# A perceiver layer's cross attention: the second of two freed context units loaded by four whole DMAs instead of some fourteen pieces

## What is computed

```python
x = x + xattn(layernorm(x), ctx)          # ctx: 8 x 1601 x 2048
x = x + attn(layernorm(x), w_q, w_k, w_v, w_o)
x = x + ffn(layernorm(x), A_w, B_w, Wq_w, keys)

def xattn(query, key):
    a = einsum('bqd,bkd->bqk', query, key)
    return einsum('bqk,bkd->bqd', softmax(a, axis=-1), key)
```

## Time and profile before

| | us |
|---|---|
| median of 3 runs | 1615.14 |
| lowest, highest run | 1612.77, 1623.99 |
| the profiled execution, its own time | 1612.68 |
| its span | 1610.9 |

### The profile page before, as it was taken

How to read it: one execution, slowest core, us unless ns; L and a number is a source line. 1 busy time by engine, 2 the same in 40 slices (tenths; PEclk the granted TensorE clock), 3 DMA queues, 4 the chain that set the end, 5 groups by cost and what they waited for, 6 DMA issues and landing times.

```text
span 1610.9 us, 24088 instructions
## 1 busy us (share of the span) xinstructions
PE 1478.6 (92%) x9593; PEld 1044.2 (65%) x9593; DVE 777.1 (48%) x1095; ACT 505.8 (31%) x698; POOL 625.3 (39%) x282
## 2 busy tenths in 40 slices
PE   1698988888889699999999999999999999999999
PEld 0233333333333388888888888888888888878777
DVE  2456646647655320446544644644465440357323
ACT  1032433433433422332423423323323332222221
POOL 0031422413405324366466564663663663430000
PEclk9899999999899799999999999999999999999999
DMA  9999899989985423233133233323331343230023
GB/s 233 247 216 227 203 255 255 216 252 254 226 238 123 139 102 108 79 105 105 56 106 98 78 104 104 102 85 99 104 104 55 106 152 105 79 105 1 29 76 131
DMA packets 182222, 219.96 MB, mean 137 GB/s; under 512 B 9488, under 2 KB 107792, under 8 KB 179504
## 3 DMA queue, kind: packets, MB, share of 16 engines
q1 hardware_dynamic: 182144, 218.87, 50.1%
HBM read 207.82 MB, written 10.49 MB: 136 GB/s over the span
## 4 chain that ended last, share of the span: by engine, by line
PE 76%; DMA 8%; DVE 6%; SPq 5%; issue 2%; ACT 2%; DVEq 0%; POOL 0%; ACTq 0%
PE ps L729 15%; PE ps L731 14%; PE ps L730 14%; PE ps L666 11%; DMA xa_raw<-in_ctx 8%; SPq L305 5%; PE ps L1769 5%; PE ps L1771 5%; PE ps L1770 5%; DVE xa_kt L520 2%; PE ps L642 2%; PE ps L1709 2%; PE ps L1862 1%; DVE xa_kt L524 1%; PE ps L1734 1%
## 5 line engine op out<-in xcount | busy, mean ns | idle before, releaser
L729 PE MATMUL ps<-h_hi,w_hi 128*128 128x512 f32 x800 | 315.4, 394 | 1.2 <-DVE h_lo L1425 1.1
L731 PE MATMUL ps<-h_hi,w_lo 128*128 128x512 f32 x800 | 311.7, 390 | 0.0
L730 PE MATMUL ps<-h_lo,w_hi 128*128 128x512 f32 x800 | 311.5, 389 | 0.0
L1157 POOL TENSOR_TENSOR w_lo<-raw,w_hi 128x2048 fp32r<-128x2048 f32 (+1 forms) x52 | 212.7, 4095 | 254.4 <-ACT w_hi L1222 213.8
L474 POOL TENSOR_TENSOR xa_x<-xa_x,xa_tmp 64x512 f32<-64x512 f32 x120 | 150.3, 1269 | 360.0 <-ACT xa_tmp L403 348.1
L622 PE MATMUL ps<-xa_kt,xa_q_t 128*64 128x416 f32 (+2 forms) x1024 | 211.1, 557 | 78.7 <-DVE xa_kt L520 56.4
L520 DVE STREAM_TRANSPOSE xa_kt<-xa_raw 128x832 f32<-128x832 f32 (+1 forms) x208 | 193.9, 995 | 158.4 <-PE ps L622 102.9
L622 PEld LDWEIGHTS ps<-xa_kt,xa_q_t 128*64 128x64 f32 x1024 | 71.8, 146 | 208.1 <-issue 134.5
L666 PE MATMUL ps<-xa_raw,xa_e_t 32*64 32x512 f32 (+1 forms) x3264 | 184.1, 593 | 0.0
L729 PEld LDWEIGHTS ps<-h_hi,w_hi 128*128 128x128 f32 x800 | 150.2, 188 | 36.4 <-issue 6.4
L1513 DVE TENSOR_TENSOR rows<-rows,ps 128x512 f32<-128x512 f32 x168 | 115.5, 688 | 116.3 <-PE ps L1771 116.3
(11 more groups left out here) (222 smaller groups left out, 1894.3 us busy)
## 6 DMA issues: line engine op xcount, KB each, us to landing
xa_raw<-in_ctx SPq DMA_DIRECT2D x128, 320.0 KB, 8.5
xa_raw<-in_ctx SPq DMA_DIRECT2D x144, 256.0 KB, 11.0
raw<-in_L_attn_w_q SPq DMA_DIRECT2D x32, 1024.0 KB, 5.9
raw<-in_L_attn_w_o SPq DMA_DIRECT2D x30, 1024.0 KB, 5.0
xa_raw<-in_ctx SPq DMA_DIRECT2D x64, 192.0 KB
xa_raw<-in_ctx SPq DMA_DIRECT2D x64, 128.0 KB
raw<-in_L_attn_w_k SPq DMA_DIRECT2D x8, 1024.0 KB, 5.2
raw<-in_L_attn_w_v SPq DMA_DIRECT2D x8, 1024.0 KB, 5.2
```

The source lines that it names most:

```text
L729: pe.matmul(out, hi, mov_hi, start=first, stop=False)
L730: pe.matmul(out, hi, mov_lo, start=False, stop=False)
L731: return pe.matmul(out, lo, mov_hi, start=False, stop=last)
L1157: pool.tensor_tensor(w_lo[:, n % 2, part], raw[:, n % 2, part], w_hi[:, n % 2, part].bitcast(F32), ALU.subtract).then_inc(w_lo_done, 1)
```

## The change

- Only units on side 1 (odd `u`) are still loaded in three pieces. A unit on side 0 (even `u`) is loaded whole: one DMA for each quadrant, four in all, counted on the third piece's semaphore. It is issued when TensorE is through with side 1 of the half batch. The order of the two (`2s+5`, then `2s+6`) stays.
- The first five units at the start follow the same rule.
- `load_rows` at half batches 5 and 9 now stands behind both units, no longer between them.
- The loader takes an engine and a queue; queue 1 (ScalarE) has no quadrants, so ScalarE issues no DMA. But the waits that go ahead of the loads are also in ScalarE's program: ahead of the copies 1, 4 and 7 of `first_half_moved` for thirds 0, 1, 2 of side 0, and ahead of `evacuate`.

```diff
-QUAD_ORDER = (0, 2, 1, 3)
+QUEUE_QUADS = ((0, 2, 1, 3), ())
+REFILL_AT = (1, 4, 7)
...
+def pieces_of(u):
+    return range(NPIECE) if u % SIDES else range(NPIECE - 1, NPIECE)
...
+def piece_runs(u, g, i):
+    n = BLOCKS[u // SIDES % HALVES]
+    if not u % SIDES:
+        return [(0, n)]
...
         for u in range(PLACES):
-            for g in range(NPIECE):
-                load_unit_piece(u, g)
+            for g in pieces_of(u):
+                load_unit_piece(sp, 0, u, g)
...
-            for a in range(SIDES):
-                u = SIDES * s + a + PLACES
-                for g in range(NPIECE):
-                    if u < UNITS:
-                        products(sp, s, g, [a])
-                        load_unit_piece(u, g)
...
+            for g in range(NPIECE):
+                u = SIDES * s + PLACES
+                if u < UNITS:
+                    products(sp, s, g, [0])
+                    load_unit_piece(sp, 0, u, g)
...
+            if SIDES * s + 1 + PLACES < UNITS:
+                products(sp, s, sides=[1])
+                load_unit_piece(sp, 0, SIDES * s + 1 + PLACES, NPIECE - 1)
+            if s >= 5 and (s - 5) % 4 == 0 and s < 10:
+                sp.wait_ge(norm_stored, 16 * ((s - 5) // 4 + 1))
+                load_rows((s - 5) // 4 + 2)
...
+        def refill(s, g):
+            u = SIDES * s + PLACES
+            if u < UNITS:
+                products(act, s, g, [0])
+                load_unit_piece(act, 1, u, g)
+
+        def refill_whole(s):
+            u = SIDES * s + 1 + PLACES
+            if u < UNITS:
+                products(act, s, sides=[1])
+                load_unit_piece(act, 1, u, NPIECE - 1)
...
             for k in range(A_OPS):
+                if k in REFILL_AT:
+                    refill(HALVES * b + 1, REFILL_AT.index(k))
...
         def evacuate(s):
             b, x = divmod(s, HALVES)
+            if x == 0:
+                for g in range(NPIECE):
+                    refill(s, g)
+            refill_whole(s)
             products(act, s)
```

More of the change, by code:

```diff
@@ L67, in place @@
     return (u + 2) % PLACES
-def piece_runs(x, g, i):
-    n = BLOCKS[x]
+def pieces_of(u):
[4 more added lines that the diff above has]
+        return [(0, n)]
     j0, j1 = PIECES[g] + i, min(PIECES[g + 1], n) + i
@@ L85, in piece_loads @@
     for v in range(u % PLACES, u + 1, PLACES):
-        n += sum(len(piece_runs(v // SIDES % HALVES, g, i)) for i in range(QUADRANTS))
+        n += sum(len(piece_runs(v, g, i)) for i in range(QUADRANTS) if g in pieces_of(v))
         n += g == NPIECE - 1 and has_left(v)
@@ L294, in part_of, with load_unit_piece @@
         return own(b) if k % 2 == 0 else other(b)
-    def cross_sync(sp, aside):
[L297 to L310, removed]
+    def load_unit_piece(eng, queue, u, g):
+        s, a = divmod(u, SIDES)
+        b, x = divmod(s, HALVES)
+        at = UNIT * place(u)
+        for i in QUEUE_QUADS[queue]:
+            for j0, j1 in piece_runs(u, g, i):
+                k0 = KEY0[x] + a * COLS[x] + SQ * j0
+                src = ctx[b, k0:k0 + SQ * (j1 - j0), i * 512:(i + 1) * 512].rearrange("(k c) n -> c k n", c=SQ)
+                eng.dma_start(raw[quadrant(i), at + j0:at + j1, :], src).then_inc(raw_in[place(u)][g], 16)
+        if queue == 0 and g == NPIECE - 1 and has_left(u):
+            if u == 2:
+                eng.wait_ge(left_clear, 1)
+            left = ctx[b, LEFT_KEY, :].rearrange("(i n) -> i n", i=QUADRANTS)
+            eng.dma_start(raw[0:P:SQ, at + LEFT_BLOCK, :], left).then_inc(raw_in[place(u)][g], 16)
+    def cross_sync(sp, aside):
         def load_rows(t):
@@ L325, in cross_sync @@
                 sp.dma_start(x1_norm[t * P:(t + 1) * P, :], xs[t % 2][:]).then_inc(norm_stored, 16)
-            for a in range(SIDES):
-                u = SIDES * s + a + PLACES
-                for g in range(NPIECE):
-                    if u < UNITS:
-                        products(sp, s, g, [a])
-                        load_unit_piece(u, g)
[L332 to L338, removed]
+            for g in range(NPIECE):
[3 more added lines that the diff above has]
+                    load_unit_piece(sp, 0, u, g)
+                if g == 0 and s >= 4 and s % 4 == 0:
+                    t = s // 4 - 1
+                    sp.wait_ge(pool_op, BATCH_OPS * (2 * t + 2))
+                    sp.dma_start(x1[t * P:(t + 1) * P, :], xs[t % 2][:]).then_inc(x1_stored, 16)
+            if SIDES * s + 1 + PLACES < UNITS:
[4 more added lines that the diff above has]
+                load_rows((s - 5) // 4 + 2)
             if s == STAGES - 3:
@@ L427, in last_moved @@
                                scale=g_b[other(b), :]).then_inc(tmp_in, 1)
+        for u in range(PLACES):
+            for g in pieces_of(u):
+                load_unit_piece(act, 1, u, g)
         normalize_rows(0)
```

## The result

| | us |
|---|---|
| kernel before, median of 4 runs | 1615.6 (1612.77 to 1623.99) |
| changed kernel, median of 4 runs | 1636.34 (1633.32 to 1638.16) |
| ratio | 1.0118, 95% interval 1.0077 to 1.0158 |
| profiled execution of the changed kernel, own time | 1638.16 |

The change costs 1.2%, about 19 us by the ratio. The prediction was 1621.8 with a range to 1630, and 0.09 for a loss of over 1%: right that it is slower, and too small by more than half.

A forecast was written before the change was run, and what follows sets the result against it. The prediction took the cross attention's loop to be bound by the landing of unit `2s+5`. It summed 1612.7 + 4.7 (rows of x) + 4.4 (clock) = 1621.8 us, other terms 0, range 1611 to 1630.

The forecast's parts named there:

- What bounds the cross attention: Cross attention: the loop closes through a DMA, since the last third of unit `2s+5` must land before VectorE's transposes.
- the sign that half batches 0 to 5 take the same time: Half batches 0 to 5 together take as long as before; otherwise a load taken as hidden is on the path.
- Fewer DMAs: SyncE's queue: 464 issues become 296, 73 us less issue time, taken at 0 because nothing on the path waits.
- Rows of `x` behind the whole unit: Half batches 6 and 10: rows land later, TensorE's queries and VectorE's transposes wait, 2.2 and 2.5 us, 4.7 together.
- The clock: TensorE in half batches 6 and 10: clock falls to 0.50 after the gaps, 2.2 us at each place, 4.4.
- ScalarE's waits: ScalarE's copies 1, 4 and 7 wait for freed thirds; taken as covered, 0, or 8 us if not.
- Speed of a whole unit: Even units loaded whole: 237 GB/s, 14.4 us for 13 blocks, taken as no change.
- Rival 3: Whole units load slower: at 200 GB/s some 18 us, 1640; decides from 217 GB/s, over 1% slower; chance 0.08.
- The second rival: Whole units load faster: at 301 GB/s 1606.7 to 1611 us, by the skill's figure 1604; chance 0.10.

The follow-up runs named there:

- e9: e6 with quadrants 0 and 1 on SyncE's queue, 2 and 3 on ScalarE's, and ScalarE's start loads reordered around its normalizations: 1571.89 us, ratio 0.9701.
- e10: e7 with the first and second thirds of the odd units also loaded in two rounds of quadrants each: 1589.90 us, ratio 0.9832.
- e11: e5 with the quadrants in the order 0, 1, 2, 3 instead of 0, 2, 1, 3, odd units too: 1636.08 us, ratio 1.0101.
- e5: e1 with each even unit in 12 DMAs, third by third, the quadrants alternating within each third: 1615.88 us, ratio 0.9998.
- e4: e1 with each even unit in 12 DMAs, a quadrant's three one behind the other: 1623.74 us, ratio 1.0039.
- e1: The changed kernel with the x rows at half batches 5 and 9 loaded between the two units again: 1619.94 us, ratio 1.0022.
- e2: The kernel before with only the x rows at half batches 5 and 9 moved behind both units: 1625.02 us, ratio 1.0059.
- e3: e1 without the waits that the change put into ScalarE's program: 1622.75 us, ratio 1.0048.
- e12: The changed kernel with each even unit in 12 DMAs, third by third, instead of 4: 1628.33 us, ratio 1.0067.
- e8: e1 reading other context bytes, rows 6 KB apart and from all four columns, written to the same places: 1617.01 us, ratio 1.0009.
- e7: e5 with the even units loaded in runs of two blocks, 28 or 24 DMAs a unit: 1609.99 us, ratio 0.9967.
- e6: e1 with quadrants 0 and 2 loaded from SyncE's queue and 1 and 3 from ScalarE's: 1633.14 us, ratio 1.0108.

## Why the prediction was right and wrong

- **What bounds the cross attention:** right. Faster landings shorten it at once (e9, e10), slower ones lengthen it (e11). But the sign that half batches 0 to 5 take the same time did not hold: in the chains the first values start 3.7 us later and those of half batch 5 5.7 us later (233.34 for 227.69). The 3.7 are the whole units of the start, which are on the path: e5, whose quadrants alternate, starts its first values within 0.2 us of before. What adds the other 2 us up to half batch 5 stays open.
- **Fewer DMAs, taken at 0:** right. The line now has 296 issues. e4 loads an even unit in the order of e1 with three times as many DMAs, and runs at the same rate.
- **Rows of `x` behind the whole unit, 4.7 + 4.4 us:** right in place and order, too small by some 5 us. The idle times were read too small: TensorE stood 8.50 and 7.23 us in e2, where I had 5.9 and 5.0. That is 4.8 us more, with the cover already used up, and makes the sum 13.9; the trace of e2 has 14.3. The failed reading is the landing. I took the rows to land 1.4 us ahead of the first DMA of the next third, since they are ahead of it in the queue. In half batch 6 of e2 that DMA was issued at 263.45 and landed 6.7 us later, at 270.2, and the rows at 270.97, behind it; why a load can land behind a DMA that was issued after it stays open. That the median of e2 gives 9.5 us and the forecast 9.1 is no confirmation: the interval, 5.0 to 14.2, holds both.
- **The clock, 4.4 of these:** it fell as forecast (0.50). But the sum did not take off the falls of before, which are gone: the last twelve score products of half batch 10 took 4.43 us at the low clock and take 2.68 in e2. What the clock alone costs was not separated.
- **ScalarE's waits, taken at 0:** right (e3, and GpSimd's unbroken pace). The 297 in that passage is nine of the 12.5 rounds, not eight; no term rests on it.
- **Speed of a whole unit, taken at 237 GB/s, "no change": this step failed.** It measured 214. That is 1.5 us a unit and 3.7 us at the start. In the total it is some 8 us by the medians of e12 and the changed kernel, and 4 by e1. In half batches 6 and 10 the traces show nothing of it on top of the rows: 14.1 us there in the changed kernel, 14.2 in e12 and 14.3 in e2. Which half batches behind the start pay the rest stays open. I took the row "with nothing but units in the queue", but every row of before has the quadrants alternating, 0, 2, 1, 3, each for 6 to 10 packets of an engine; the change makes it 26 packets in a row, and no row bore on that. Against the slow side I set that no stretch was under 232, which was no evidence for the same reason. And I argued from the DMA share of 1.06 that nothing can be lost: the share is 1.07 at 214, 1.05 at 302 (e10, 36 to 46 us) and 1.05 at 378 GB/s. It tells that the engines are occupied, not how much they move.
- **Rival 3** had the sign, the start and nearly the point (217 GB/s) and 0.08 of the chance. By its own scale (18 us at 200) 214 makes about 10, with the 9.1 of the rows 1632. That this is near the measured time is in part luck: its 2.7 us on the rows in each of half batches 6 and 10 do not show, and the rows cost more than 9.1. Its "same stretch of columns" was half right: it is the stretch of partitions, not of the source (e8).
- **The second rival**, and the rule of large DMAs that I weighed for it, fell the other way: the kernels with the smallest pieces (e7, e10) are faster than that with the largest (e1). The prediction also left half of the rule out: the row of the Trainium skill, page "DMA: Bandwidth & Descriptors", section "Rules for kernel authors", has 128 partitions beside the 1 MiB. Each DMA of a whole unit here writes 32.

## What to carry to other kernels

Before pieces are merged or reordered, ask what alternates between them: here the small DMAs were fast because their destinations changed, and their size made hardly any difference (e1, e4). A full share of the DMA engines is no sign that they are at their best; compare the GB/s at that share with the best stretch of the same trace (301 in half batch 8), and ask what is different there. And a load that is put behind another inherits its lateness: follow who waits for it, down to the next engine that stands.

## What the runs showed of the hardware

DMAs into the same 32 partitions, one behind the other, moved 214 GB/s as four long DMAs a unit and 217 as twelve (e1, e4). Two queues, one on partitions 0 to 31 and one on 32 to 63, moved 218 over 6 to 12 us and 226 over 6 to 20 us (e6); on halves 64 partitions apart 370 to 378 (e9). In one queue, the order 0, 1, 2, 3 gave 221 (e11) and 0, 2, 1, 3 gave 237 (e5), and 265 with shorter runs (e7).

The Trainium skill has this on the page "SBUF — State Buffer", section "Door 1: The DMA port swizzle": partitions 0 to 31 reach 8 of 16 ports, 32 to 63 the same eight, 64 to 127 the other eight, with some 218 GB/s for eight. The runs agree with it in which quadrants help each other and, at 214 to 218, in the figure; the ports themselves show in no view, so the mechanism is the page's and not shown here. It is the page that the prediction should have weighed. The next section there, "Can I just issue two DMAs to hit both halves?", says that two DMAs on the two halves gain only 6% over one. Here the measurement is another, and it decides: 214 with one quadrant at a time (e1), 370 to 378 with one in each half from two queues (e9), and 265 from one queue whose DMAs alternate (e7).
